# Gated delta rule on Trainium2: PE computes the outputs of a 128-token tile from the state at its start, VectorE only updates the state

## The reference

```python
q = (x @ Wq + bq).reshape(batch, seq, H, D)      # H = D = 16; k and v likewise
k = k / (norm(k) + 1e-06)
beta = sigmoid(x @ Wbeta + bbeta)
def _step(Sm, inputs):                            # for each token, batch and head
    q_t, k_t, v_t, beta_t = inputs
    Sk = einsum('bhde,bhe->bhd', Sm, k_t)
    delta = v_t - Sk
    Sm = Sm + beta_t[..., None] * einsum('bhd,bhe->bhde', delta, k_t)
    o_t = einsum('bhde,bhe->bhd', Sm, q_t)
    return (Sm, o_t)
return outputs @ Wo + bo
```

## Time and profile before

| | us |
|---|---|
| median of three executions | 5755.36 |
| profiled execution | 5748.21 |
| its span, first to last instruction | 5746.9 |
| PE busy (share of the span) | 4334.5 (75%) |
| VectorE (DVE) busy | 4153.2 (72%) |
| ScalarE (ACT) busy | 1945.3 (34%) |
| GpSimd (POOL) busy | 872.5 (15%) |

### The profile page before, as it was taken

How to read it: one execution, slowest core, us unless ns; L and a number is a source line. 1 busy time by engine, 2 the same in 40 slices (tenths; PEclk the granted TensorE clock), 3 DMA queues, 4 the chain that set the end, 5 groups by cost and what they waited for, 6 DMA issues and landing times.

```text
span 5746.9 us, 70671 instructions
## 1 busy us (share of the span) xinstructions
PE 4334.5 (75%) x23962; PEld 3031.9 (53%) x23962; DVE 4153.2 (72%) x9356; ACT 1945.3 (34%) x4665; POOL 872.5 (15%) x1159
## 2 busy tenths in 40 slices
PE   6322078977889768887899978886889688977875
PEld 3101055655666546665667755653566455655553
DVE  1999999999999999998354565665566566655533
ACT  3111022221222111111132355653666455645442
POOL 1010011010111000000000001024100322023434
PEclk8655589999999989999899988997999899988887
DMA  2210000000000000000000001121111223122445
GB/s 76 115 40 7 0 10 11 13 4 13 6 12 12 4 12 8 8 4 28 12 1 5 12 19 60 47 63 64 52 49 52 79 79 96 55 76 74 146 149 161
DMA packets 192498, 249.28 MB, mean 43 GB/s; under 512 B 25744, under 2 KB 169744, under 8 KB 191888
## 3 DMA queue, kind: packets, MB, share of 16 engines
q1 hardware_dynamic: 167568, 177.63, 9.5%
q0 software_dynamic: 24576, 67.14, 3.7%
HBM read 120.94 MB, written 123.73 MB: 43 GB/s over the span
## 4 chain that ended last, share of the span: by engine, by line
PE 41%; DVE 38%; issue 10%; POOL 5%; ACT 4%; DMA 2%; SPq 0%; DVEq 0%; ACTq 0%; POOLq 0%
PE psum L956 7%; DVE rec L1200 5%; DVE rec L1213 4%; DVE rec L1202 4%; DVE skb L1205 4%; DVE rec L1216 4%; PE psum L973 4%; POOL xbuck L1850 3%; PE psum L1131 3%; PE psum L987 3%; DVE region L1208 2%; PE psum L1045 2%; PE psum L894 2%; PE psum L1028 2%; PE psum L1030 2%
## 5 line engine op out<-in xcount | busy, mean ns | idle before, releaser
L956 PE MATMUL psum<-xnT,w_w13T 128*128 128x256 f32 x4352 | 1068.1, 389 | 0.0
L956 PEld LDWEIGHTS psum<-xnT,w_w13T 128*128 128x128 f32 x4352 | 840.0, 195 | 146.1 <-issue 27.4
L973 PE MATMUL psum<-w_w2T,hid 128*128 128x256 f32 x2176 | 620.9, 409 | 234.3 <-DVE hid L1292 221.3
L1367 DVE TENSOR_REDUCE region<-psum 128x1 f32<-128x384 f32 (+3 forms) x704 | 429.2, 637 | 317.5 <-PE psum L1011 307.1
L1637 ACT ACTIVATE sil<-psum 128x256 f32<-128x256 f32 x408 | 156.4, 383 | 1378.7 <-PE psum L956 1360.6
L1154 DVE SCALAR_TENSOR_TENSOR sil<-sil,psum 128x128 f32<-128x128 f32 (+1 forms) x504 | 165.5, 328 | 563.1 <-ACT sil L1734 354.1
L973 PEld LDWEIGHTS psum<-w_w2T,hid 128*128 128x128 f32 x2176 | 378.9, 192 | 357.1 <-DVE hid L1292 276.8
L1693 ACT ACTIVATE region<-psum 128x512 f32<-128x512 f32 (+3 forms) x1024 | 407.8, 439 | 215.6 <-PE psum L1032 205.5
L1131 PE MATMUL psum<-w_w13T,region 128*128 x1344 | 385.0, 412 | 14.4 <-ACT region L1728 10.1
L1213 DVE TENSOR_TENSOR rec<-ub,region 128x512 f32<-128x512 f32 x512 | 378.0, 738 | 8.0
L882 PE MATMUL psum<-w_ident,xn 128*128 128x128 f32 x512 | 95.8, 318 | 368.3 <-ACT xn L1542 365.1
(11 more groups left out here) (228 smaller groups left out, 8309.3 us busy)
## 6 DMA issues: line engine op xcount, KB each, us to landing
ybuck<-region SPq DMA_DIRECT2D x336, 128.0 KB
region<-xbuck SPq DMA_DIRECT2D x202, 128.0 KB, 2.2
xbuck<-x SPq DMA_DIRECT2D x40, 512.0 KB, 5.3
scale<-xbuck SPq DMA_DIRECT2D x134, 128.0 KB, 2.2
x_scratch<-x SPq DMA_DIRECT2D x16, 512.0 KB, 3.2
x_scratch<-region SPq DMA_DIRECT2D x32, 256.0 KB, 2.2
region<-x_scratch SPq DMA_DIRECT2D x64, 128.0 KB, 2.8
out<-region SPq DMA_DIRECT2D x64, 128.0 KB
```

The costliest lines, as they stand in the source:

```text
L956: o = e.matmul(psum[:, gi, m * 256:m * 256 + 256], w13T[:, x, k, m * 128:(m + 1) * 128], xnT[xi][:, k, cols], start=(k == 0), stop=(k == 1 ...
L973: o = e.matmul(psum[:, yi, j * D:(j + 1) * D], hid[hi][:, j * 128:(j + 1) * 128], w2T[:, x, :], start=(x == 0 and j == 0), stop=(x == NX - ...
L1367: e.tensor_reduce(mx[:, qt, h0:h0 + nh], psum[:, mi, 0:nh * n].rearrange("p (a k) -> p a k", a=nh), AX.X, ALU.max, negate=True).then_inc(s ...
```

## The change

VectorE keeps five of the seven operations of a step; the difference `v - S k` is now written over v, in `vo`, so that after 128 steps `vo` holds the corrections u of the tile. With the state S0 at the start of the tile, the output of token t is

o_t = S0 q_t + sum over s <= t of (k_s . q_t) u_s

and PE computes it in `first_rows`, for a row (one batch, 128 tokens) in four *quads* of four heads:

- `a_dot`: four products k q^T (128 x 128 each) with the 32 partitions of two heads; the q of the other head of a pair is zero in its copy.
- `a_mask`: VectorE multiplies the four with a triangle of ones, from PSUM to SBUF.
- `a_value`: four products of the corrections (16 columns of weights) with the masked matrices, each to its own 32 partitions of a bank; from the second quarter on four more with the old state.
- `a_out`: ScalarE copies the bank to SBUF. `o_proj` has four products in place of two, with a Wo that has zero rows in the gaps.

For this q and k are also needed with channels on partitions. `p_q` computes q in that layout directly (ScalarE adds the bias and makes the two copies with zeros, L1631 of the changed kernel), `k_turn` and `k_out` transpose the normalised k; both go to DRAM (`qT_scratch`, `kT_scratch`) and `o_in` loads a row's 128 KB and 256 KB of them beside x. At the end of a quarter `state` copies the state (ScalarE), SP stores it, and `state_in` loads it for the next rows. `l_turn` has 16 groups in place of 24, `o_turn`, `o_copy` and `step_out` are gone. Square and sum of k are four pairs over adjacent elements. FFN_RATE is 0.45 (0.40), PROJECT_RATE 0.2 (0.15).

```diff
-FFN_RATE, PROJECT_RATE, LAST_RATE = 0.40, 0.15, 0.4
+FFN_RATE, PROJECT_RATE, LAST_RATE = 0.45, 0.2, 0.4
...
+            for i in range(4):
+                mi, mf = yield from misc.take()
+                put("k_turn", 4 * k + i, mi, mf)
+                yield LIGHT
+                put("k_out", 4 * k + i, mi)
+                misc.give(mi, "kte", 4 * k + i + 1)
+                yield LIGHT
...
+            def quad(a):
+                mi, mf = yield from misc.take()
...
+                put("a_dot", a, qi, t_ql, mi, mf)
+                yield LIGHT
+                pi, pf = yield from wts.take()
...
+                put("a_mask", t_dot, mi, pi, pf)
+                yield LIGHT
+                yield LIGHT
...
+                put("a_value", q, n, j, a, qi, t_mask, mi, pi)
+                wts.give(pi, "apv", t_pv)
+                yield LIGHT
...
+                put("a_out", a, t_pv, mi, ti, tf)
+                misc.give(mi, "aout", nth["aout"])
+                yield LIGHT
+
+            yield from staggered([quad(a) for a in range(4)], 1)
...
-        for i in range(24):
+        for i in range(16):
             mi, mf = misc.get()
             put("l_turn", q, i, mi, mf)
...
-        put("step_out", q)
+        if q + 1 < NQ:
+            put("state", q)
...
+            elif name == "a_dot":
+                a, qi, t_ql, mi, mf = u
+                rows_a = slice(32 * a, 32 * a + 32)
+                pe.wait_ge(s[f"ql{qi}"], t_ql)
+                pe.wait_ge(s[mf[0]], mf[1])
+                for c in range(4):
+                    o = e.matmul(psum[:, mi, c * 128:(c + 1) * 128], kTl[qi][rows_a, c // 2, :],
+                                 qTl[qi][rows_a, c % 2, c // 2, :], start=True, stop=True, skip_group_check=True)
+                o.then_inc(s["adot"], 1)
+            elif name == "a_value":
...
+                for c in range(4):
+                    hh = 16 * (2 * a + c % 2 + c // 2 * 8)
+                    o = e.matmul(psum[32 * c:32 * c + 16, mi, 0:128], x1[n][:, j, hh:hh + 16], wts[pi][:, c, :],
+                                 start=True, stop=(q == 0), skip_group_check=True)
+                if q:
+                    pe.wait_ge(s["S0"], 16 * q)
+                    for c in range(4):
+                        o = e.matmul(psum[32 * c:32 * c + 16, mi, 0:128], S0[rows_a, 2 * (4 * n + j) + c // 2, :],
+                                     qTl[qi][rows_a, c % 2, c // 2, :], start=False, stop=True, skip_group_check=True)
+                o.then_inc(s["apv"], 1)
...
                     e.tensor_tensor(tk[:, :, :, :], S[:, :, :, :], ktt, ALU.mult).then_inc(s["scan"], 1)
-                    if t:
-                        e.tensor_tensor(tq[:, :, :, :], S[:, :, :, :], bc(kq[:, :, t - 1, 16:32], 2, 16),
-                                        ALU.mult).then_inc(s["scan"], 1)
                     dv.wait_ge(s["scan"], c + 1)
                     e.tensor_reduce(skb[:, :, :], tk[:, :, :, :], AX.X, ALU.add).then_inc(s["scan"], 1)
-                    if t:
-                        dv.wait_ge(s["scan"], c + 2)
-                        e.tensor_reduce(vo[:, :, t - 1, :], tq[:, :, :, :], AX.X, ALU.add).then_inc(s["scan"], 1)
...
+            elif name == "k_out":
+                i, mi = u
+                ac.wait_ge(s["ktt"], i + 1)
+                ac.wait_ge(s["ks"], 16 * i)
+                e.activation(kTs, psum[:, mi, :].rearrange("p (b k t) -> p b k t", b=2, k=2), ACT.Copy).then_inc(s["kte"], 1)
...
+            elif name == "state_in":
+                q, = u
+                sp.wait_ge(s["Sx"], 16 * q)
+                sp.wait_ge(s["apv"], 64 * q)
+                e.dma_start(S0, S_dram[q - 1].rearrange("(i h e d) -> (h e) i d", i=32, h=8, e=16)).then_inc(s["S0"], 16)
```

324 lines of the change are left out of this document (205 added, 119 removed).

## The result

The changed kernel takes 5993.71 us (median of four runs, 5987.05 to 5997.19), the kernel before on the same chip 5755.03. The ratio is 1.0412, 95% interval 1.0394 to 1.043: slower by 4.1%, 239 us. The forecast was 5865 us, slower by 1.9%; the direction and the range held, the size was half of what came (116 us for 239).

A forecast was written before the change was run, and what follows sets the result against it. VectorE was taken to bound the kernel, PE 110 to 140 us behind in three of four quarters, then PE the later quarters. From 5748: -120 - 21 + 5 + 93 + 10 + 149 = +116, 5865 us; range 5690 to 6040.

The forecast's parts named there:

- VectorE's step, -120: First quarter, where nothing else binds: each of 128 steps falls from 4.07 to 3.13 us, -120 us.
- quarter ends, -21: At four quarter ends, 8 of 24 transpose groups (3.8 us) and step_out (1.4 us) go, -21 us.
- The start, +5: Before the first step: k transposes and kTs stores added, square and sums of k cheaper; net +5 us, bounds -5 and +20.
- A quad, 2.0 us (1.6 without the old state): PE's price for four heads of one tile, including 0.25 us for switches; bounds 1.3 and 3.5 us.
- Dear switches: Rival: each change of shape on PE costs 0.3 us more, three per quad; 6065 us, chance 0.12.
- Cheap quads by overlap of neighbours: Rival: neighbouring quads overlap on PE and switches cost nothing, 1.3 us a quad; 5705 us, chance 0.20.
- The later quarters, +93: Second to fourth quarter: PE, not VectorE, ends last; 662, 700 and 620 us against 645, 645 and 599; +93 us.
- S0 +103: Later quarters' +93 with +10 us for loading the old state in 64-byte pieces, +5 in each of two quarters.
- its share between steps 16 and 96 of the third quarter: Sign: PE busy over 93% there, VectorE under 85% and waiting for PE.
- The tail, +149: After the last step: quads 128, o_proj 28, start 15 us, in place of 22 us; +149, bounds +95 and +270.
- half clock: Rival: tail and each quarter's first 16 steps at 1.2 GHz, tail +120, quarters +20 each; 6045 us, chance 0.12.
- The side: Whole kernel: slower 0.69, faster 0.23, same 0.08; hangs on the quad's price, with the sum zero at 1.55 us.

The follow-up runs named there:

- e5: Changed kernel with the k q^T products of two quads alternating, neighbours in different partition groups and banks, FFN_RATE 0.55; ratio 1.0404 to the kernel before.
- e3: Changed kernel without the four products with the old state in each quad (that part of the outputs missing); 5911.72 us, ratio 1.0269.
- e11: Changed kernel with ScalarE copying the four matrices of a quad in place of VectorE's mask, triangle left out; 5980.28 us, ratio 1.0394.
- e1: Kernel before with only VectorE's output operations (L1202, L1208, step_out) removed, scan outputs not computed; 5389.48 us, ratio 0.9358.
- e2: Changed kernel with two VectorE operations put back in each step, their result read by nobody; 6272.45 us, ratio 1.0896.
- e9: Changed kernel with the first block's rows and head counted for half, FFN_RATE 0.40 and PROJECT_RATE 0.15; 5963.23 us, ratio 1.0365.
- e6: Changed kernel with SP issuing a row's k and q loads ahead of the wait for x's buffer; ratio 1.0305 to the kernel before.
- e4: Changed kernel with one more unread 256-column whole-array product on PE behind each quad of the tail; 5961.11 us, ratio 1.0354.
- e10: Changed kernel with e5's pairs, five tail banks, q and k loaded before x, row shares altered, rates 0.40 and 0.15; 5863.51 us, ratio 1.0187.
- e12: Kernel before with GpSimd making the product of state and query in the first quarter, VectorE summing it; ratio 0.9981.

## Why the prediction was right in direction and half the size

*VectorE's step, -120, and quarter ends, -21.* Right: -117 for the first quarter with its end, where the table has -121, and -8.5 for the three turns, where it has -11.

*The start, +5.* Wrong sign, small: the first step comes 9.6 us earlier, of which the forecast has 3.8 for the eight groups fewer in l_turn. Which edit brings the other 6 was not taken apart.

*A quad, 2.0 us (1.6 without the old state).* At 2.4 GHz it is 1.76 (1.42). The price was set from L1045 and a full-array transpose, plus 0.25 for switches; a switch costs at most 0.1. That settles two rivals. Dear switches (0.3 each): refuted. Cheap quads by overlap of neighbours: little of it in the order that the change writes, where each a_dot has other work around it or its own group beside it; e5 shows that the overlap is there once neighbours differ in group and bank, and is then worth half of a_dot.

*The later quarters, +93, with S0 +103: came +154.* The step that failed is the idle time in the sum, not the work. The forecast was made on stretches of 645, 645 and 599 us that leave out the last 10 to 16 us of each quarter, 13, 12 and 6 us of PE's busy time in them. Over the whole quarters, with modelled ends, it says 655, 682 and 601 us of PE's busy time and leaves 23, 33 and 29 us in which PE is idle (in the third: the 45 that I added for the uneven list and for stops, less 15 that the profile counts as busy in modelled ends, plus 3 in the part left out). The busy time came at 636, 676 and 600, a little less than forecast since a quad is cheaper than 2.0; the idle time came at 62, 55 and 56, 88 us more in all. That PE would end last was right (e3 against e11), and so was its share between steps 16 and 96 of the third quarter:

```profile
1383.00:1916.00 533.00, 508.96 (x2924) 377.88 (x2925) 366.06 (x784) 122.24 (x298) 55.39 (x81) 0.94 0.09 28
```

There PE is busy 95% and VectorE 69%. More than half of the idle time lies outside, in the first 16 and the last 32 steps. By PE's waits (the longest stand with the profile after), 12 of the 55 us end with the quarter's last steps, 8 with a layer norm, 8 with the routing of the blocks, 4 with a load of q, and 15 with a unit's gate (L1364), spread over 19 waits: the handover between the two engines at each unit, which I put at 10, is the smaller part. e1 has the same 56 us in its second quarter with no quad in the kernel (21 of them behind the unit's gate), and e2 has 96 with both engines at about 670, 40 of them there. So the quads did not make the idle time; it came on top of the new sum. e9 takes 8 to 11 us of it off each quarter by sharing the work out otherwise. For the +10 of S0 no wait of PE for the state shows in its list.

A low clock at the head of a quarter is no new cost: from 598 to 680 us the changed kernel is granted 0.73, the kernel before 0.72 in the first 80 us of its second quarter.

*The tail, +149: came +221.* "Nothing lies beside it" was right, and that PE bounds it as well. The price of the products was wrong, and this is the second step that failed. The forecast took 2.4 GHz, since L926 ran at 0.43 us for 256 columns at this place before. But that row shows 22 us of whole-array transposes and products, with 0.94 granted; with the quads in their place the granted clock is 0.60. The quads came to 159 us for 128 and o_proj to 56 for 28, and 27 us of waits stand where 15 were forecast for the start: 31, 28 and 12 or so make the 72 us. This was the rival "half clock", which named 120 us for the tail and had 0.12; 72 came. The waits for q and k come from the order of SP's list (e6), which the forecast did not walk through although it says that a row's loads are issued there. The two hang together: without the waits the clock was granted more (0.64) and 24 us of busy time went too. e4 and e6 stand for 33 and 62 us; they were not run together.

*The side.* With a quad at 1.76 us (1.42 without the old state) the sum by my own working would have been 5865 - 192 x 0.24 - 64 x 0.18, about 5807, still slower. The dear quads and a start that came 10 us earlier hid a part of the error in the idle time; the range held by that luck too.

## What to carry to other kernels

Work that is moved off a recurrence has to be priced where it lands last: here 117 us came back in the only quarter where VectorE stood alone, and 221 went to the rows behind the last step, which nothing covers. Where two engines are both busy for most of a stage, the larger of the two sums is not reached: 47 to 62 us in a quarter came on top in the changed kernel, e1, e9 and e11, 96 in e2. Look for it at the head and the end of the stage and at the routing of each block, and not only at the handover of each unit. Small products should be written so that neighbours use different row groups and different banks (e5), with the list shared out anew for it, or the time does not come back (e5 against e10), and the queue that loads their operands should meet the wait that frees first before the one that frees last.

## What the runs showed of the hardware that was not expected

- Products with 32 rows of weights in one group run one behind the other (four in 1.08 us at 2.4 GHz), in two groups and two banks fully side by side (eight in 1.09).
- At 1.2 GHz the same four take 2.0 us; but twelve of three quads in a row took 4.03 us there and 2.6 at 2.4 GHz, so the products at a change of groups overlap at either clock, where three times four one behind the other would be 6.0 and 3.2:

```profile
2722.21 4.03 PE L978 MATMUL psum<-region 32*128 32x128 f32 x24
```

- PE busy 221 of 250 us, with quads of 16-column or 32-row products and o_proj behind every fourth, was granted 0.60 of the clock; with one whole-array product of 256 columns behind each quad 0.85 (e4).
- A product of two SBUF operands on GpSimd beside VectorE's takes 1.77 us for 512 numbers, and a VectorE operation of 32 numbers at its end takes 0.42 us in place of 0.19 (e12).
